# Filter stage: the other half's ten columns, dealt out in runs of lines instead of by rows

## The chip, the cores and the metric

The kernel runs on one core of a Trainium2 chip. The metric is the time of one execution on the device, in microseconds (us); several executions are timed and the median is given. Engines are named as in the profile: PE (TensorE), DVE (VectorE), ACT (ScalarE), POOL (GpSimd) and SP (SyncE, here the main issuer of DMAs). PEld is the loading of weights into TensorE.

## What is computed

The input is `x` of 16 samples, 32 channels and 64 x 64 pixels. Four residual layers follow each other, each on a group-normalised copy of `x`: an attention layer with 3x3 and 7x7 convolutions, a convolution quantised to 8 bits, a depthwise 3x3 convolution with kernels made from the pooled input, and an oriented filter. The change lies in the last one. Cut to that layer:

```python
center_k, surround_k = _make_kernels()      # 8 orientations each, 21 x 21 Gaussians, sigma 3.65 and 3.65/8; surround 3 times wider
tidx = jnp.arange(16) % 8                   # sample n has orientation n % 8
center_resp   = per_sample_conv(x, center_k[tidx])
surround_resp = per_sample_conv(x, surround_k[tidx])
return jnp.maximum(center_resp - lstd * surround_resp, 0.0)   # lstd: scaled local deviation of x
```

Every channel of a sample is convolved with the same 21x21 kernel, so a pixel needs the values up to ten rows and ten columns away.

## The kernel before, in words

**Layout.** Partitions hold 4 image rows modulo 4 (G) times 32 channels; the free dimension holds the 16 samples. The filter stage turns this around: for each sample the image is transposed into `xt[s]`, where the 128 partitions are 4 rows x 32 columns (one half of the width), and the free dimension holds half, high and low part (each value is two float16), 22 row blocks of 4 rows (16 real ones and 3 of padding on each side) and 32 channels. A filter is then a set of matmuls. The weights, 128 x 128, say how the pixels of one block of 4 rows x 32 columns enter the pixels of another, and one matmul applies them to up to 16 row blocks x 32 channels = 512 columns. Three matmuls (high x high, high x low, low x high) make one product of nearly float32 precision.

**Windows.** The weights come in ten windows for each kernel (centre and surround, `f`) and orientation `t`. Windows 0 to 4 are the own half, row blocks -2 to 2 (`rows_of`, L1747). Window 5 is the outer rows, from the tile `outer`. Windows 6 to 9 are the neighbour columns: of the other half, the ten columns next to the border reach over, with seven row blocks. These are 240 pairs of row and column for each half; they are gathered in the tile `edges[s]` as two parts of 120 partitions, near and far (windows 6 and 7 for half 0, 8 and 9 for half 1; `rest_of`, L1757). In the kernel before, the near part is row blocks 1 to 3 and the far part is 4, 5, half of 6 and half of 0, each with all ten columns, in every orientation. A window whose weights are all zero is skipped (`filled`, L1749 and L1760).

**How the edges come there.** The ten columns lie on other partitions, and each is needed shifted by several row blocks. So `store_edges` (L481) writes them with 8 DMAs of 10 partitions to the DRAM tensor `edge_columns`, as 40 lines (row of the block x column) per half, and `load_edges` (L496) or `load_right` (L1365) reads them back with 7 DMAs per half, of 40 or 20 lines, each line as two pieces of 1 KB. `copy_outer` (L490) fills `outer` with 2 DMAs.

**Order of the work.** Samples are taken in the order n = 2t + s: the two samples of orientation t, then the next orientation. Everything with index s has two buffers. TensorE's `filters(t, s)` (L1738) does the rows of both kernels and halves, waits for `outer`, the left and the right edges, and then does the rest. The last sample is split by halves. VectorE transposes (`turn_in`), makes the low part (`low`) and combines the results (`combine`); ScalarE makes the high part (`high`), normalises and takes roots. `high` for sample n waits until sample n - 2 is filtered.

**The DMA queues.** SP issues, in order: the table of orientation 0 and then, for sample 0, stores, outer copies and the loads of *both* halves (L536 to L539), the same for sample 1 (L542), and the table of orientation 1 (L543). Then a loop (L545) over orientations: for s = 0 and 1 `prefetch(t + 1, s)`, which loads only the left half, and `store_out(t, s)`; then `load_tables(t + 2)`. From orientation 1 on the right half is loaded by ScalarE's own DMA queue, in `load_right`, which stands between ScalarE's activations in its loop (L1397). A DMA issued there holds up the activations behind it. TensorE waits on counts of DMAs, 16 for each (L1773 to L1775).

Of the kernel before, what the change touches and what calls it, by code (L numbers as in the profile page):

```python
# [20 lines left out]
B, C, H, W = 16, 32, 64, 64  # L21
P = 128
G = 4
NY = H // G
# [15 lines left out]
KSZ, NT = 21, 8  # L40
NH = W // 2
YP, YN = 3, NY + 6
# [8 lines left out]
NREAL = 12 * NBW  # L51

KB, KQ, KV, KK = range(4)
NSIDE, NCENT = 256, 640


def host_constants():
# [15 lines left out]
    j, wi = p // NBW, p % NBW  # L73
    real = p < 12 * NBW
    rows_in, cols_in, used = [], [], []
    for d in range(-2, 3):
        rows_in.append(4 * d + r), cols_in.append(w), used.append(p >= 0)
    rows_in.append(np.where(r < 2, 12 + r, r - 12)), cols_in.append(w), used.append(p >= 0)
    neighbour_rows = np.array([[4 * a + q - 12 for a in (1, 2, 3) for q in range(4)],
                               [4 * a + q - 12 for a in (4, 5) for q in range(4)] + [12, 13, -10, -9]])  # L80
    for hf in range(2):
        for part in range(2):
            rows_in.append(neighbour_rows[part][np.minimum(j, 11)])
            cols_in.append(NH + wi if hf == 0 else wi - NBW)
            used.append(real)
    tab = np.zeros((NT, P, 2, NWIN, 2, P), np.float16)
    for t in range(NT):
        th = float(np.float32(t * np.pi / NT))
        xr = xx * np.cos(th) + yy * np.sin(th)
        yr = -xx * np.sin(th) + yy * np.cos(th)  # L90
        for cs, m in enumerate((1.0, 3.0)):
            k = np.exp(-0.5 * (xr * xr / (3.65 * m) ** 2 + yr * yr / (3.65 / 8 * m) ** 2))
            k = k / k.sum() * TS
            for v in range(NWIN):
                dh = rows_in[v][:, None] - r[None] + 10
                dw = cols_in[v][:, None] - w[None] + 10
                ok = (dh >= 0) & (dh < KSZ) & (dw >= 0) & (dw < KSZ) & used[v][:, None]
                m_ = np.where(ok, k[np.clip(dh, 0, 20), np.clip(dw, 0, 20)], 0.0)
                hi = m_.astype(np.float16)
                tab[t, :, cs, v, 0] = hi  # L100
                tab[t, :, cs, v, 1] = (m_ - hi.astype(np.float64)).astype(np.float16)
# [32 lines left out]
def program(nc, x, conv_w, pack, m1, mb1, dyn_w, cf, ch, tables, out):  # L134
# [3 lines left out]
    with ctx:  # L138
# [248 lines left out]

        @block.sync
        def _(sp):
# [91 lines left out]
            def store_edges(t, s):  # L481

                wait_alone(sp, g.xl, 2 * t + s + 1)
                for h, w0 in ((0, 0), (1, NH - NBW)):
                    for r in range(G):
                        sp.dma_start(edge_dram[s, h, NBW * r:NBW * r + NBW],
                                     xt[s][NH * r + w0:NH * r + w0 + NBW, 1 - h].rearrange("p l y c -> p l (y c)")
                                     ).then_inc(edge_out[s], 16)
# [7 lines left out]
            def load_edges(t, s, halves=(0,)):  # L496
                sp.wait_ge(edge_out[s], 128 * (t + 1))
                for h in halves:
                    for part, at_, r0, n, a in ((0, 0, 0, 4, 1), (0, 4, 0, 4, 2), (0, 8, 0, 4, 3),
                                                (1, 0, 0, 4, 4), (1, 4, 0, 4, 5), (1, 8, 0, 2, 6), (1, 10, 2, 2, 0)):  # L500
                        sp.dma_start(edges[s][NBW * at_:NBW * (at_ + n), part, h],
                                     edge_dram[s, h, NBW * r0:NBW * (r0 + n), :, C * a:C * (a + NY)]
                                     ).then_inc((edge_in if h == 0 else right_in)[s], 16)
# [41 lines left out]
            with sp.Fori(0, (NT - 2) // 2) as t2:  # L545
                for slot in range(2):
                    t = 2 * t2 + slot
                    for s in range(2):
                        prefetch(t + 1, s)
                        store_out(t, s)  # L550
                    load_tables(t + 2, slot)
# [602 lines left out]
        def _(a):  # L1154
# [210 lines left out]
            def load_right(t, s):  # L1365
                a.wait_ge([g.edge_out0, g.edge_out1][s], 128 * (t + 1))
                for part, at_, r0, n, y in ((0, 0, 0, 4, 1), (0, 4, 0, 4, 2), (0, 8, 0, 4, 3),
                                            (1, 0, 0, 4, 4), (1, 4, 0, 4, 5), (1, 8, 0, 2, 6), (1, 10, 2, 2, 0)):
                    a.dma_start(edges[s][NBW * at_:NBW * (at_ + n), part, 1],
                                edge_dram[s, 1, NBW * r0:NBW * (r0 + n), :, C * y:C * (y + NY)]  # L1370
                                ).then_inc([g.right_in0, g.right_in1][s], 16)
# [25 lines left out]
            with a.Fori(0, NT - 2) as t:  # L1397
# [85 lines left out]
        def _(pe):  # L1483
# [254 lines left out]
            def filters(t, s):  # L1738
# [18 lines left out]
                def rest_of(f, hf):  # L1757
                    for window, src in ((5, outer[s][:, hf]), (6 + 2 * hf, edges[s][0:NREAL, 0, hf]),
                                        (7 + 2 * hf, edges[s][0:NREAL, 1, hf])):
                        if not filled[t, f, window]:  # L1760
                            continue
                        for lt, lx in ((0, 0), (0, 1), (1, 0)):
                            rows = src.shape[0]
                            last = mm(bank[4 * s + 2 * f + hf], tb[0:rows, f, window, lt], src[:, lx],  # L1764
                                      start=False, stop=(window == 7 + 2 * hf and lt == 1), skip_group_check=True)
# [8 lines left out]
                pe.wait_ge([g.edge_in0, g.edge_in1][s], 16 * 7 * (t + 1))  # L1774
                pe.wait_ge([g.right_in0, g.right_in1][s], 16 * 7 * (t + 1))  # L1775
# [77 lines left out]
```

## Time and profile before

| | |
|---|---|
| median of 3 runs | 1197.33 us (1196.41 to 1201.05) |
| the profiled execution's own time | 1200.27 us |
| its span, first to last instruction | 1197.3 us |
| mean granted TensorE clock | 0.961 of full speed |
| TensorE matmul busy | 90% of the span |
| VectorE, ScalarE, GpSimd busy | 68%, 45%, 27% |
| filter stage on the chain of waits | from 887.6 us to the end |

Busy shares are averages over five stages with different limits; for one stage the chain of waits and the stretches are to be read. Times in the trace count from the first instruction. A DMA's row on a queue (SPq, ACTq) is the time for which the issuing queue was taken up, not the transfer.

### The profile page before, as it was taken

To read this page: it belongs to the slowest core of one execution; us is meant where nothing else is said; L and a number is where in the kernel's file an instruction comes from. 1 tells how busy PE (TensorE), PEld (TensorE's weight loads), DVE (VectorE), ACT (ScalarE), POOL (GpSimd) and SP (SyncE) were. 2 spreads that over 40 slices of the span, in tenths; PEclk is the share of its full clock that TensorE was granted. 3 is DMA by queue.
4 is the path that set the end of the run, shared out by engine and by line. 5 is a ranking of instruction groups with operands and counts; after the bars stand their busy time and mean duration, and the time that the engine had idled before them with its cause. 6 is when DMAs were issued, how large, how long until landed. Compare 5 with 4: busy or idle time off the path is not lost.

```text
span 1197.3 us, 38501 instructions
## 1 busy us (share of the span) xinstructions
PE 1076.6 (90%) x17036; PEld 790.9 (66%) x17036; DVE 808.9 (68%) x1001; ACT 537.1 (45%) x747; POOL 321.8 (27%) x364
## 2 busy tenths in 40 slices
PE   2999999999999999999923589978989999999997
PEld 2999989999899999999821245433334444444443
DVE  6456585684857848477296978689989645466444
ACT  3524635546364563625334967677941212121110
POOL 1374545535464363545410000022300000000000
PEclk9999999999999999999956988989989999999999
DMA  6020020200202000010001444322354654566551
GB/s 210 7 77 3 3 76 3 76 3 3 76 3 76 3 18 27 3 42 3 3 1 37 105 104 112 91 59 71 93 140 124 190 171 117 171 178 187 152 139 43
DMA packets 52115, 89.77 MB, mean 75 GB/s; under 512 B 8795, under 2 KB 36699, under 8 KB 50940
## 3 DMA queue, kind: packets, MB, share of 16 engines
q1 hardware_dynamic: 44264, 80.56, 24.3%
q10 hardware_dynamic: 7700, 6.89, 2.0%
q8 instruction: 133, 2.18, 0.7%
q14 instruction: 18, 0.15, 0.0%
HBM read 36.89 MB, written 11.99 MB: 41 GB/s over the span
## 4 chain that ended last, share of the span: by engine, by line
PE 74%; DVE 17%; ACT 3%; issue 3%; DMA 2%; SPq 1%; DVEq 0%; ACTq 0%
PE psum L1519 38%; PE psum L1753 16%; PE psum L1764 10%; PE psum L1653 5%; DVE small L711 2%; PE psum L1555 2%; DMA arena<-arena 2%; DVE arena L1008 1%; DVE small L586 1%; DVE X L904 1%; PE psum L1568 1%; DVE arena L1027 1%; DVE arena L1015 1%; PE psum L1541 1%; DVE arena L1021 1%
## 5 line engine op out<-in xcount | busy, mean ns | idle before, releaser
L1519 PE MATMUL psum<-arena 128*128 128x64 f16 (+2 forms) x11904 | 514.9, 207 | 22.3 <-DMA arena<-arena 12.6
L1519 PEld LDWEIGHTS psum<-arena 128*128 128x128 f16 x11904 | 497.8, 99 | 38.2 <-issue 12.7
L625 DVE TENSOR_TENSOR arena<-psum,arena 128x512 f32<-128x512 f32 x128 | 87.9, 691 | 170.0 <-PE psum L1519 142.4
L1753 PE MATMUL psum<-arena 128*128 128x512 f16 (+2 forms) x936 | 192.4, 366 | 0.0
L1753 PEld LDWEIGHTS psum<-arena 128*128 128x128 f16 x936 | 92.2, 99 | 98.7 <-issue 3.3
L1431 POOL TENSOR_SCALAR arena<-arena,constants_f 128x256 f16<-128x256 f16 x126 | 138.6, 1128 | 0.0
L1427 POOL TENSOR_TENSOR arena<-arena 128x256 f16<-128x256 f32 x63 | 51.7, 820 | 309.5 <-ACT arena L1189 309.5
L1184 ACT ACTIVATE arena<-arena 128x256 f16<-128x256 f32 x63 | 26.5, 420 | 208.4 <-issue 105.5
L1764 PE MATMUL psum<-arena 120*128 120x512 f16 (+1 forms) x528 | 116.9, 379 | 0.0
L1764 PEld LDWEIGHTS psum<-arena 120*128 120x128 f16 (+1 forms) x528 | 51.4, 97 | 61.8
L1475 POOL TENSOR_TENSOR arena<-arena 128x1024 f32<-128x1024 f32 x16 | 30.4, 1899 | 206.8 <-ACT arena L1331 153.9
L1653 PE MATMUL psum<-arena 128*32 128x512 f16 x1152 | 69.6, 404 | 6.3 <-DMA arena<-arena 6.3
L1188 ACT ACTIVATE arena<-arena,small,constants_f 128x256 f16<-128x256 f32 x126 | 74.9, 663 | 0.0
L1043 DVE TENSOR_TENSOR arena<-arena 128x1024 f16<-128x1024 f32 x16 | 19.6, 1223 | 74.9 <-ACT arena L1359 74.6
L1363 ACT ACTIVATE arena<-arena 128x1024 f32<-128x1024 f32 x16 | 16.9, 1057 | 109.3 <-DVE arena L1051 109.3
L1359 ACT ACTIVATE arena<-arena 128x1024 f16<-128x1024 f32 x16 | 16.9, 1055 | 108.3 <-PE psum L1764 97.3
L1653 PEld LDWEIGHTS psum<-arena 128*32 128x32 f16 x1152 | 32.4, 101 | 42.0 <-DMA arena<-arena 7.7
L1432 POOL TENSOR_TENSOR arena<-arena 128x256 f32 (+1 forms) x63 | 55.7, 884 | 0.0
L1210 ACT ACTIVATE arena<-arena,small,constants_f 128x2048 f16<-128x2048 f32 x14 | 37.7, 2757 | 37.7 <-DVE arena L683 37.7
L688 DVE SCALAR_TENSOR_TENSOR arena<-arena,constants_f 128x2048 f16<-128x2048 f32 x14 | 38.2, 2730 | 15.7 <-ACT arena L1210 15.7
L1702 PE MATMUL psum<-arena,constants_f 128*128 128x512 f16 x192 | 47.0, 397 | 0.6 <-DVE arena L1008 0.4
L1555 PE MATMUL psum<-arena 128*128 128x64 f16 x768 | 25.8, 198 | 21.5 <-DVE arena L666 21.5
(209 smaller groups left out, 1413.3 us busy)
## 6 DMA issues: line engine op xcount, KB each, us to landing
arena<-in_filter_tables SPq DMA_DIRECT2D x8, 1280.0 KB, 8.6
arena<-arena SPq DMA_DIRECT2D x32, 264.0 KB, 3.9
X<-in_x SPq DMA_DIRECT2D x16, 512.0 KB, 4.7
arena<-arena SPq DMA_DIRECT2D x32, 256.0 KB, 4.0
out<-X SPq DMA_DIRECT2D x16, 512.0 KB, 4.0
arena<-edge_columns SPq DMA_DIRECT2D x90, 80.0 KB
arena<-edge_columns ACTq DMA_DIRECT2D x70, 80.0 KB
arena<-arena SPq DMA_DIRECT2D x32, 140.0 KB, 2.5
```

The costliest lines, as they stand in the source:

```text
L625: v.tensor_tensor(out_, bank_rows(k), biasrow, ALU.add).then_inc([g.staged0, g.staged1][k], 1)
L688: v.scalar_tensor_tensor(PX[1][:, :, :, s], p_ch, smask[s], PX[0][:, :, :, s], ALU.mult, ALU.subtract).then_inc(g.pl_ready, 1)
L1188: a.activation(k_rows(0, y2, s), chunk(y2, KK), ACT.Identity, scale=smask[s], bias=zero1)
L1427: gp.tensor_tensor(khl[:, y2 % 2, 1], chunk(y2, KK), khl[:, y2 % 2, 0], ALU.subtract).then_inc(g.klow, 1)
L1431: gp.tensor_scalar(k_rows(1, y2, s), khl[:, y2 % 2, 1], smask[s], None, ALU.mult)
L1432: gp.tensor_tensor(v_rows(1, i, y2), chunk(y2, KV), v_rows(0, i, y2), ALU.subtract).then_inc(g.lo_ready, 1)
L1519: last = mm(conv[k][:, c0:c1], win[:, kk, lx, y + e, dx:dx + W, :].rearrange("p w s -> p (w s)"), wt[:, lw, d, w0:w1], start=(n == 0), sto ...
L1555: last = mm(att[:, H * c:H * c + H], PX[lp][:, c].rearrange("p h s -> p (h s)"), VV[lv][:, kk * C + c], start=(c % 8 == 0 and n == 0), sto ...
L1653: last = mm(slot_banks(B + n)[hf][C * row:C * row + C, :], kw[:, lw, row, dx], src[:, k, lx, 8 * hf + e:8 * hf + e + 8, dx:dx + W], start= ...
L1702: mm(bank[4 * k + hf], near, wx3[k][:, l, 8 * hf:8 * hf + 8, dx:dx + W], start=(dx + l == 0), stop=False, skip_group_check=True)
L1753: mm(bank[4 * s + 2 * f + hf][:, C * lo:C * hi], tb[:, f, d + 2, lt], xt[s][:, hf, lx, YP + d + lo:YP + d + hi].rearrange("p y c -> p (y c)"),
L1764: last = mm(bank[4 * s + 2 * f + hf], tb[0:rows, f, window, lt], src[:, lx], start=False, stop=(window == 7 + 2 * hf and lt == 1), skip_gr ...
```

## The change

The 40 lines of a half are put into `edge_columns` by column first in orientations 0, 1 and 7 (`BY_COLUMN`), by row otherwise, and in orientations 5 to 7 with the rows mirrored. For each orientation a table (`EDGE_NEAR`, `EDGE_FAR`; orientations 5 to 7 use those of 3 to 1, mirrored) says which runs of lines of which row block belong to the near part and which to the far part. A part has 112 to 128 rows instead of 120. In orientations 2 and 6 the division stays as before. The loads follow the tables, one DMA for each entry; an entry with five numbers gathers several short runs in one DMA with a source of four levels. TensorE's waits count the loads so far. Since the number of loads differs from one orientation to the next, the loops over orientations on SP and ScalarE are written out.

```diff
+BY_COLUMN = (0, 1, 7)
+EDGE_NEAR = {
+    0: ((1, 0, 20), (2, 0, 20), (3, 0, 20), (4, 0, 20), (5, 0, 20), (0, 2, 2, 0, 5), (6, 0, 2, 0, 5)),
+    1: ((1, 0, 8), (2, 0, 12), (3, 0, 20), (4, 0, 28), (5, 0, 30), (6, 0, 2, 0, 7)),
+    2: ((1, 0, 40), (2, 0, 40), (3, 0, 40)),
+    3: ((2, 20, 15), (3, 0, 40), (4, 0, 40), (5, 0, 30)),
+    4: ((2, 10, 30), (3, 0, 40), (4, 0, 40), (5, 0, 10)),
+}
+EDGE_FAR = {
+    0: ((1, 20, 20), (2, 20, 20), (3, 20, 20), (4, 20, 20), (5, 20, 20), (0, 2, 2, 5, 5), (6, 0, 2, 5, 5)),
+    1: ((0, 2, 2, 0, 10), (1, 8, 32), (2, 12, 28), (3, 20, 20), (4, 28, 12), (5, 30, 10), (6, 0, 2, 7, 3)),
+    2: ((4, 0, 40), (5, 0, 40), (6, 0, 20), (0, 20, 20)),
+    3: ((0, 20, 20), (1, 0, 40), (2, 0, 20), (2, 35, 5), (5, 30, 10), (6, 0, 20)),
+    4: ((0, 20, 20), (1, 0, 40), (2, 0, 10), (5, 10, 30), (6, 0, 20)),
+}
+
+def edge_line(t, row, column):
+    row = G - 1 - row if t > NT // 2 else row
+    return G * column + row if t in BY_COLUMN else NBW * row + column
...
+        def edge_pieces(t, s, h):
+            line = 2 * YN * C
+            for k, part in enumerate(edge_parts(t, h)):
+                at_ = 0
+                for a, lines in part:
+                    n = sum(len(run) for run in lines)
+                    src = edge_dram[s, h, lines[0][0]:lines[0][-1] + 1, :, C * a:C * (a + NY)]
+                    if len(lines) > 1:
+                        src = bass.AP(edge_dram.tensor, src.offset,
+                                      [[G * line, len(lines)], [line, len(lines[0])], [YN * C, 2], [1, C * NY]])
+                    yield edges[s][at_:at_ + n, k, h], src
+                    at_ += n
+
+        def edge_loads(t, h):
+            return 16 * sum(len(part) for turn in range(t + 1) for part in edge_parts(turn, h))
...
-                        sp.dma_start(edge_dram[s, h, NBW * r:NBW * r + NBW],
+                        first, last = edge_line(t, r, 0), edge_line(t, r, NBW - 1)
+                        sp.dma_start(edge_dram[s, h, first:last + 1:(last - first) // (NBW - 1)],
...
-                    for part, at_, r0, n, a in ((0, 0, 0, 4, 1), (0, 4, 0, 4, 2), (0, 8, 0, 4, 3),
-                                                (1, 0, 0, 4, 4), (1, 4, 0, 4, 5), (1, 8, 0, 2, 6), (1, 10, 2, 2, 0)):
-                        sp.dma_start(edges[s][NBW * at_:NBW * (at_ + n), part, h],
-                                     edge_dram[s, h, NBW * r0:NBW * (r0 + n), :, C * a:C * (a + NY)]
-                                     ).then_inc((edge_in if h == 0 else right_in)[s], 16)
+                    for dst, src in edge_pieces(t, s, h):
+                        sp.dma_start(dst, src).then_inc((edge_in if h == 0 else right_in)[s], 16)
...
-            with sp.Fori(0, (NT - 2) // 2) as t2:
-                for slot in range(2):
-                    t = 2 * t2 + slot
-                    for s in range(2):
-                        prefetch(t + 1, s)
-                        store_out(t, s)
-                    load_tables(t + 2, slot)
+            for t in range(NT - 2):
+                for s in range(2):
+                    prefetch(t + 1, s)
+                    store_out(t, s)
+                load_tables(t + 2, t % 2)
...
+                for dst, src in edge_pieces(t, s, 1):
+                    a.dma_start(dst, src).then_inc([g.right_in0, g.right_in1][s], 16)
...
-            with a.Fori(0, NT - 2) as t:
+            for t in range(NT - 2):
...
-                    for window, src in ((5, outer[s][:, hf]), (6 + 2 * hf, edges[s][0:NREAL, 0, hf]),
-                                        (7 + 2 * hf, edges[s][0:NREAL, 1, hf])):
-                        if not filled[t, f, window]:
-                            continue
+                    near, far = (edge_count(part) for part in edge_parts(t, hf))
+                    used = [v for v in (5, 6 + 2 * hf, 7 + 2 * hf) if filled[t, f, v]]
+                    for window in used:
+                        rows = {5: P, 6 + 2 * hf: near, 7 + 2 * hf: far}[window]
+                        src = outer[s][:, hf] if window == 5 else edges[s][0:rows, (window - 6) % 2, hf]
...
-                pe.wait_ge([g.edge_in0, g.edge_in1][s], 16 * 7 * (t + 1))
-                pe.wait_ge([g.right_in0, g.right_in1][s], 16 * 7 * (t + 1))
+                pe.wait_ge([g.edge_in0, g.edge_in1][s], edge_loads(t, 0))
+                pe.wait_ge([g.right_in0, g.right_in1][s], edge_loads(t, 1))
```

An entry of three numbers is (row block, first line, lines); one of five is (row block, first row, rows, first column, columns). The weights in the tables of constants are arranged to match.

## Rows read from the trace of the kernel before

**Rows 1.** The page, part 1: busy time, share of the span, instructions of each engine.

```profile
PE 1076.6 (90%) x17036; PEld 790.9 (66%) x17036; DVE 808.9 (68%) x1001; ACT 537.1 (45%) x747; POOL 321.8 (27%) x364
```

**Rows 2.** The chain that ended last, in time order: start us, us, what.

```profile
887.61 14.24 PE psum L1753 x60
901.85 7.79 PE psum L1764 x36
...
929.41 11.99 PE psum L1753 x60
941.40 7.78 PE psum L1764 x36
...
1020.50 6.48 PE psum L1764 x30
...
1038.98 6.49 PE psum L1764 x30
...
1187.44 3.90 PE psum L1764 x18
```

**Rows 3.** Stretches of the filter stage: first and last of five of 50 us.

```profile
core 0: us, PE busy (x) PEld busy (x) DVE busy (x) ACT busy (x) POOL busy (x), PEclk, DMA share, GB/s
900.00:950.00 50.00, 50.00 (x243) 23.57 (x242) 39.36 (x54) 7.64 (x8) 0.00 (x0) 1.00 0.52 140
...
1100.00:1150.00 50.00, 50.00 (x244) 23.72 (x243) 25.32 (x23) 7.54 (x7) 0.00 (x0) 1.00 0.55 158
```

**Rows 4.** Timeline of SP's queue, samples 0 and 1: start us, us, what.

```profile
888.09 11.70 SPq L501 DMA_DIRECT2D arena<-edge_columns  x14
899.99 2.92 SPq L486 DMA_DIRECT2D edge_columns<-arena  x8
902.96 1.43 SPq L492 DMA_DIRECT2D arena<-arena  x2
```

**Rows 5.** Groups by line and shape, from 860 us: count | busy us, mean ns.

```profile
L1764 PE MATMUL psum<-arena 120*128 120x512 f16 x384 | 91.8, 379 | 0.0
...
L1764 PE MATMUL psum<-arena 128*128 128x512 f16 x144 | 39.0, 379 | 0.0
```

**Rows 6.** L501: all durations, then its fifth to eighth issue alone.

```profile
L501 SPq DMA_DIRECT2D arena<-edge_columns x126: 769/781/1076, 888.1 to 1164.0; - x126
...
891.60 0.77 SPq L501 DMA_DIRECT2D arena<-edge_columns  x1
...
892.42 0.78 SPq L501 DMA_DIRECT2D arena<-edge_columns  x1
...
893.24 0.77 SPq L501 DMA_DIRECT2D arena<-edge_columns  x1
...
894.06 0.78 SPq L501 DMA_DIRECT2D arena<-edge_columns  x1
```

**Rows 7.** Other lines of SP's queue: ns min/median/max; under L520, L478 their landing.

```profile
L486 SPq DMA_DIRECT2D edge_columns<-arena x128: 281/329/1682, 882.6 to 1156.9; - x128
...
L520 SPq DMA_DIRECT2D arena<-arena x128: 548/591/1309, 780.8 to 881.9; - x128
...
DMA to landing us min/median/max: 1.9/2.0/5.8
...
L478 SPq FUSED_REGOPS  x6: 43/43/43, 949.4 to 1126.0; - x6
...
DMA to landing us min/median/max: 5.5/8.6/9.7
```

**Rows 8.** Stretches around the first filter matmul; columns as in rows 3.

```profile
882.00:886.50 4.50, 0.23 (x2) 0.00 (x0) 0.63 (x1) 1.26 (x2) 0.00 (x0) 0.86 0.90 303
886.50:891.80 5.30, 5.23 (x13) 1.94 (x14) 4.01 (x4) 0.00 (x0) 0.00 (x0) 0.50 0.60 140
```

**Rows 9.** Timeline of one sample's round on ScalarE: start us, us, what.

```profile
1008.61 1.06 ACT L1359 ACTIVATE arena<-arena 128x1024 f16<-128x1024 f32 x1 [10.31 <-PE psum L1764]
...
1017.03 1.06 ACT L1363 ACTIVATE arena<-arena 128x1024 f32<-128x1024 f32 x1 [6.23 <-DVE arena L1051]
...
1017.03 5.62 ACTq L1369 DMA_DIRECT2D arena<-edge_columns  x7
```

More of the change, by code:

```diff
@@ L50, with edge_parts, edge_count, edge_rows @@
 NPS = 3
-NREAL = 12 * NBW
 KB, KQ, KV, KK = range(4)
 NSIDE, NCENT = 256, 640
+BY_COLUMN = (0, 1, 7)
+EDGE_NEAR = {
[5 rows of a table added]
+}
+EDGE_FAR = {
[5 rows of a table added]
+}
+def edge_line(t, row, column):
+    row = G - 1 - row if t > NT // 2 else row
+    return G * column + row if t in BY_COLUMN else NBW * row + column
+def edge_parts(t, hf):
+    parts = []
+    for part in (EDGE_NEAR[min(t, NT - t)], EDGE_FAR[min(t, NT - t)]):
+        pieces = []
+        for a, *of in part:
+            if len(of) == 2:
+                lines = [range(of[0], of[0] + of[1])]
+                if hf:
+                    lines = [range(40 - of[0] - of[1], 40 - of[0])]
+            else:
+                r0, c0 = of[0], of[2]
+                if hf:
+                    r0, c0 = G - of[0] - of[1], NBW - of[2] - of[3]
+                lines = [range(G * c + r0, G * c + r0 + of[1]) for c in range(c0, c0 + of[3])]
+            pieces.append((6 - a if (t > NT // 2) != (hf == 1) else a, lines))
+        parts.append(pieces)
+    return parts
+def edge_count(part):
+    return sum(len(run) for a, lines in part for run in lines)
+def edge_rows(t, part):
+    place = {edge_line(t, q, c): (q, c) for q in range(G) for c in range(NBW)}
+    at = [(4 * (a - 3) + place[n][0], place[n][1]) for a, lines in part for run in lines for n in run]
+    return np.array(at).T
 def host_constants():
@@ L72, in host_constants @@
     r, w = p // NH, p % NH
-    j, wi = p // NBW, p % NBW
-    real = p < 12 * NBW
     rows_in, cols_in, used = [], [], []
@@ L78, in host_constants @@
     rows_in.append(np.where(r < 2, 12 + r, r - 12)), cols_in.append(w), used.append(p >= 0)
[L79 to L85, printed above, removed]
     tab = np.zeros((NT, P, 2, NWIN, 2, P), np.float16)
@@ L90, in host_constants @@
         yr = -xx * np.sin(th) + yy * np.cos(th)
+        del rows_in[6:], cols_in[6:], used[6:]
+        for hf in range(2):
+            for part in edge_parts(t, hf):
+                rows, cols = edge_rows(t, part)
+                unused = np.zeros(P - len(rows), int)
+                rows_in.append(np.concatenate([rows, unused]))
+                cols_in.append(np.concatenate([cols, unused]) + (NH if hf == 0 else -NBW))
+                used.append(p < len(rows))
         for cs, m in enumerate((1.0, 3.0)):
@@ L1366, in load_right @@
                 a.wait_ge([g.edge_out0, g.edge_out1][s], 128 * (t + 1))
[L1367 to L1371, printed above, removed]
+                for dst, src in edge_pieces(t, s, 1):
+                    a.dma_start(dst, src).then_inc([g.right_in0, g.right_in1][s], 16)
             a.wait_ge(g.zero3, 1)
@@ L1757, in rest_of @@
                 def rest_of(f, hf):
-                    for window, src in ((5, outer[s][:, hf]), (6 + 2 * hf, edges[s][0:NREAL, 0, hf]),
-                                        (7 + 2 * hf, edges[s][0:NREAL, 1, hf])):
-                        if not filled[t, f, window]:
-                            continue
+                    near, far = (edge_count(part) for part in edge_parts(t, hf))
[3 more added lines that the diff above has]
+                        src = outer[s][:, hf] if window == 5 else edges[s][0:rows, (window - 6) % 2, hf]
                         for lt, lx in ((0, 0), (0, 1), (1, 0)):
-                            rows = src.shape[0]
                             last = mm(bank[4 * s + 2 * f + hf], tb[0:rows, f, window, lt], src[:, lx],
-                                      start=False, stop=(window == 7 + 2 * hf and lt == 1), skip_group_check=True)
+                                      start=False, stop=(window == used[-1] and lt == 1), skip_group_check=True)
                     return last
```

## The prediction

> **What bounds the kernel now.** I read the page first. TensorE is busy 90% of the span [rows 1], so the question is what it does in the stage that the change touches, and whether it ever waits there. The chain of waits in order of time answers both: from 887.61 to 1191.34 us it holds nothing but filter matmuls, L1753 and L1764 by turns, one pair for each of fifteen samples and two for the last, which is split by halves [rows 2]. Between 900 and 1150 us every 50 us stretch has 50.00 us of TensorE, at a granted clock of 1.00 (2.4 GHz), while VectorE has 25 to 39 us, ScalarE under 8 and the DMA engines a share of about 0.5 (first and last of the five stretches [rows 3]). So a matmul less is time less, for as long as everything that feeds the matmuls stays early. The feeders were read next, in the timeline of SP's queue, since it is SP that brings the neighbour columns. At the start of the stage SP has no slack at all: it issues sample 0's fourteen edge loads from 888.09 for 11.70 us, to 899.79, and TensorE wants them at 901.85 [rows 2, 4].
>
> **What goes.** With the columns dealt out in runs, the centre kernel of six orientations (0, 1, 3, 4, 5, 7) has no weight in the far window. I counted this from the formula of the kernels: before, all four edge windows of both kernels held weights in all eight orientations. A window costs three matmuls, there are two halves, so a sample of these orientations loses 6, twelve samples lose 72. The chain gives 36 matmuls of L1764 in 7.78 us and 30 in 6.48 [rows 2]: 0.216 us each, 1.30 per sample, **15.6 us** in all, and all of it on the path. The rows of a matmul change from 120 to between 112 and 128; with 120 and with 128 one reads 379 ns [rows 5], so this costs nothing.
>
> **What comes: loads.** The bytes are the same (240 rows of two 1 KB pieces per half). The number of loads is not: counted from the tables, a half takes 14, 13, 7, 10, 9, 10, 7, 13 loads in orientations 0 to 7, where each took 7. What does an issue cost? L501 has 126, with 769/781 ns at least and in the median [rows 6]. The decisive reading is that this doesn't follow the size: of SP's first seven, the fifth moves 40 rows and takes 0.77 us, the sixth and the seventh move 20 rows and take 0.78 and 0.77, the eighth has 40 again and 0.78; from start to start it is 0.82 [rows 6]. In orientation 0, 10 of the 14 loads of a half are exactly this 20-row form. The other four gather 10 rows in five runs, a four-level source that no row shows. From below it is bounded by a store of 10 rows, 329 ns, from above by the dearest L501, 1076 ns [rows 6, 7]; I take 0.83 us from start to start as for the others, being the nearest in direction and shape.
>
> **What comes: the stores.** Still 8 per sample, 10 rows each, but in orientations 0, 1 and 7 the DRAM side is strided. Now 329 ns (2.92 us for 8). A gain is excluded, for the rows and bytes are the same. From above, a 32-row copy strided on both sides takes 591 ns [rows 7], which is 0.26 more each. I take 0, as the nearest row is the store itself, and keep up to 2.1 us per sample for the range.
>
> **The loops that go.** SP's and ScalarE's loops over orientations become straight code. A register instruction between the issues takes 43 ns [rows 7]; I cost it at nothing. What hides it is the slack of both queues in the steady stage, reckoned below.
>
> **On the path: the start of the stage.** Both halves of samples 0 and 1 are loaded by SP alone, so SP issues 28 loads where it issued 14, twice. By the trace's own clock:
> - Sample 0: 28 loads from 888.09 end near 911.4; the last starts at 910.5 and lands 2.0 us later (the median of the nearest copies, L520 [rows 7]), at 912.5. TensorE, ready at 901.85, waits about 10.7 us.
> - The clock then falls. After the idle stretch from 882 to 886.5 us, the granted clock was 0.50 (1.2 GHz) for 886.5 to 891.8 [rows 8], and the first 60 filter matmuls took 14.24 us where later ones take 11.99 [rows 2]: 2.3 us lost. I take 2.3 for each stall, and 0 to 3 for the range. Sample 0 ends at 912.5 + 6.5 + 2.3 = 921.3, and sample 1's own rows are done at 933.3.
> - SP goes on only now: 8 stores and 2 copies of sample 1 (2.92 + 1.43 us [rows 4]) from 911.5, the wait for their landing (0.4), and 28 loads from 916.3 to 939.5, landed at 940.7. TensorE waits 7.4 us. The loss of the first stall is inside this one: the path is SP's.
> - Sample 1 ends at 940.7 + 6.5 + 2.3 = 949.5. Before, sample 2 began at 929.41 [rows 2]. **Behind by 20.1 us**, the two samples' own saving counted already.
>
> **Behind it.** Table 1 is issued at 939.8 and takes 8.6 us (9.7 at most [rows 7]): 948.4, just ahead of 949.5. Sample 2's 13 loads per half come from both queues in parallel: SP 940.2 + 2.9 + 1.4 + 0.5 + 13 x 0.87 = 956.3, landed 957.6, wanted at 949.5 + 12.0 = 961.5. ScalarE's `high` for sample 3 stands behind its own 13 issues and comes at 955.8, not 949.5; VectorE's low half, the combination of sample 1, the clamp and the root follow, as now in 8.4 us from 1008.61 to 1017.03 [rows 9], then 13 issues of 0.80, landed near 977, wanted at 980. Table 2 would be there at 983.7, wanted at 986.5. Three covers of 3 to 4 us each; none gives way by these numbers.
>
> In steady state ScalarE's round, `high` to the last load, is 14.0 us with 7 issues (1008.61 to 1022.65 [rows 9]) and 14.0 + 0.80 x 3 or 6 with 10 or 13, so 16.4 and 18.8. Samples last 17.2 to 19.8 us, but only 13.6 in orientation 4. There ScalarE falls behind by some 2 to 6 us; the loads it issues until 1022.65 land some 2 us later and are wanted at 1038.98 [rows 2, 9], 14 us later still, so TensorE doesn't see it. SP's round is 4.4 + 0.9 + 13 x 0.87 + 0.8 = 17.4 us at most, below ScalarE's.
>
> **Sum.** +20.1 from samples 0 and 1, -13.0 from the other ten samples: **+7.1 us**. The sum is made against the profiled execution, whose span is 1197.3 and whose time is 1200.27 us, 2.9 above the median of the three runs, 1197.33. I add the difference to the median: 1204.4.
>
> **A rule against the reading.** A 20-row load holds its queue for 0.78 us [rows 6]. The Trainium skill, "DMA: Bandwidth & Descriptors", section "Issuing engines are not separate DMA queues", says that the time on the sequencer to start a DMA is usually small relative to the DMA itself, and its section "Anatomy of one DMA" puts the dispatch at about 50 ns within a fixed cost that is mostly completion. By it twice as many loads would cost nothing, and the time would be 1181.7. This trace speaks against that for this form of load.
>
> **Rivals.**
> 1. *Issue time follows the size, so nothing is late.* Half-size loads at half the time keep SP's 11.7 us per sample; the whole 15.6 us is gained: 1197.3 - 15.6 = **1181.7**. For it: stores of 10 rows take 329 ns. Against: 20 and 40 rows alike. This is the rival of the other side; it decides when a 20-row load costs under some 0.45 us. 0.12. The skill's rule above gives the same end.
> 2. *The unseen four-level loads are cheap.* At 0.37 us from start to start, 8 in each set of 28 save 3.7 us, 7.4 over the two sets: 1197.0, **no change**. For it the stores' 10 rows, against it that rows haven't mattered so far. 0.14.
> 3. *The start is dearer and drags a second thing along.* Strided stores at 0.59 (+4.2 us) and four-level loads at 1.08 (+0.25 x 16 = +4) put SP 8 us later, table 1 with it: **1212**; and the covers of 3 us at samples 3 and 4 go. 0.14.
> 4. *That the change doesn't do what it says* (the far window still filled) is excluded by the count.
>
> **Chances.** Forecast 0.60, the rivals 0.12, 0.14, 0.14. A measurement here tells 0.5%, 6 us: faster is below 1191.3, slower above 1203.3. The forecast has a width of about 3 us around 1204.4, so 0.18 of its 0.60 counts as no change; of rival 2's 0.14, 0.12 does. Faster 0.12; same 0.18 + 0.12 = 0.30; slower 0.42 + 0.02 + 0.14 = 0.58. The range leaves out rival 1 and reaches from rival 2 to rival 3 with its own spread: 1196 to 1214.
>
> **What would show it.** In the profile after: L1764's successor with 1392 - 936 = 456 matmuls; TensorE waiting on a DMA of the edge tiles twice, by 11 and 7 us, ahead of samples 0 and 1, with the clock at half after each; SP's load line with 56 issues before table 1, over 23 us per set; no wait of TensorE from sample 2 on. Wrong it is if SP's loads in that place are clearly under 0.77 us, or if a third wait stands among the samples.

## The result, and the profile after

The changed kernel takes 1210.53 us in the median (1207.9 to 1216.49, 7 runs), beside 1196.41 for the kernel before (1191.15 to 1201.05, 7 runs): a ratio of 1.0134, 95% interval 1.0098 to 1.0169, so 12 to 20 us slower. (The ratio is that of the compared sets of runs; the quotient of the two medians is 1.0118. The same holds for the experiments below, each of which was compared with runs of the kernel before taken beside it.) The forecast was 1204.4, 7.1 us more than before, in a range of 1196 to 1214. The sign is as forecast, and so is the mechanism at the start of the stage; the loss is about twice what was summed, because further waits came behind the start.

Where one execution is compared with another I use the filter stage alone, from the start of its first matmul to the start of its last: 887.4 to 1190.9 before, 880.0 to 1202.3 after, **303.5 and 322.3 us**. The code ahead of it is the same in both, and yet the profiled executions of all the kernels here reach it between 880.0 and 887.4 us; that scatter of 7 us is in the spans, but not in the stage. Each kernel was profiled once, so how much the stage itself varies from one execution to the next was not measured.

The page, part 1, of the changed kernel (as rows 1):

```profile
PE 1057.1 (87%) x16964; PEld 777.3 (64%) x16964; DVE 809.0 (67%) x1001; ACT 537.1 (44%) x747; POOL 322.8 (27%) x364
```

72 matmuls fewer, as counted (17036 - 16964), but TensorE's share fell from 90% to 87%. The stretches of its filter stage (columns as in rows 3) say where it now stands still:

```profile
core 0: us, PE busy (x) PEld busy (x) DVE busy (x) ACT busy (x) POOL busy (x), PEclk, DMA share, GB/s
900.00:950.00 50.00, 37.09 (x155) 16.29 (x156) 21.88 (x38) 4.51 (x5) 0.00 (x0) 0.82 0.36 97
950.00:1000.00 50.00, 45.44 (x211) 20.97 (x210) 28.62 (x26) 9.74 (x9) 0.00 (x0) 0.93 0.55 153
1000.00:1050.00 50.00, 50.00 (x244) 23.63 (x243) 26.30 (x24) 8.67 (x8) 0.00 (x0) 1.00 0.56 167
...
1100.00:1150.00 50.00, 48.00 (x234) 22.62 (x233) 29.92 (x27) 9.74 (x9) 0.00 (x0) 1.00 0.60 168
```

The timeline of SP's queue, ScalarE's queue (ACTq) and TensorE at the start of the stage; the bracket is TensorE's idle time and what ended it (as rows 4; L1814 is `rows_of`, L1825 `rest_of`, L569 and L1432 are the loads, L555 the stores, L561 the outer copies, L546 the tables):

```profile
880.42 23.50 SPq L569 DMA_DIRECT2D arena<-edge_columns  x28
904.45 3.10 SPq L555 DMA_DIRECT2D edge_columns<-arena  x8
905.62 9.49 PE L1825 MATMUL psum<-arena 128*128 128x512 f16 x30 [11.45 <-DMA arena<-edge_columns]
...
909.07 23.67 SPq L569 DMA_DIRECT2D arena<-edge_columns  x28
914.94 12.15 PE L1814 MATMUL psum<-arena 128*128 128x512 f16 x60
...
932.79 0.43 SPq L546 DMA_DIRECT2D arena<-in_filter_tables  x1
933.36 3.42 SPq L555 DMA_DIRECT2D edge_columns<-arena  x8
934.39 8.76 PE L1825 MATMUL psum<-arena 128*128 128x512 f16 x30 [7.29 <-DMA arena<-edge_columns]
936.83 1.43 SPq L561 DMA_DIRECT2D arena<-arena  x2
940.59 11.03 SPq L569 DMA_DIRECT2D arena<-edge_columns  x13
940.60 11.53 ACTq L1432 DMA_DIRECT2D arena<-edge_columns  x13
...
954.98 6.65 PE L1825 MATMUL psum<-arena 128*128 128x512 f16 x30
...
960.65 11.05 ACTq L1432 DMA_DIRECT2D arena<-edge_columns  x13
...
970.99 0.71 SPq L546 DMA_DIRECT2D arena<-in_filter_tables  x1
...
978.18 9.05 PE L1825 MATMUL psum<-arena 128*128 128x512 f16 x30 [4.56 <-DMA arena<-edge_columns]
```

28 loads take 23.50 and 23.67 us of SP where 14 took 11.70. TensorE waits 11.45 us in sample 0, 7.29 in sample 1, and again, unforeseen, 4.56 in sample 3. The 30 matmuls behind each of these waits take 9.49, 8.76 and 9.05 us; undisturbed, in sample 2, they take 6.65. That is the clock: in the changed kernel's stretches around the first wait (PEclk is the granted clock),

```profile
900.00:905.50 5.50, 0.00 (x0) 0.00 (x0) 5.50 (x6) 0.00 (x0) 0.00 (x0) 0.50 0.17 43
905.60:911.00 5.40, 5.38 (x13) 1.89 (x14) 4.17 (x22) 0.73 (x2) 0.00 (x0) 0.50 0.53 115
911.00:915.00 4.00, 4.00 (x19) 1.76 (x18) 2.06 (x2) 0.53 (x1) 0.00 (x0) 0.95 0.32 81
```

TensorE is idle in the first, runs at 0.50 (1.2 GHz) in the second, 13 matmuls in 5.4 us, and is nearly back at full speed in the third (0.95). Two later waits complete the list, in the timeline of TensorE: at sample 12, for its table, and at the last sample.

```profile
1124.74 12.15 PE L1814 MATMUL psum<-arena 128*128 128x512 f16 x60 [2.00 <-issue]
...
1190.08 3.40 PE L1825 MATMUL psum<-arena 128*128 128x512 f16 x15 [1.15 <-DMA arena<-edge_columns]
```

The first of these two has no releaser in the trace. That it is the table is worked out: SP issues the table of orientation 6 at 1113.97, the longest time from issue to landing of any table here is 10.7 us, and TensorE goes on at 1124.74.

The account: 303.5 - 15.6 (matmuls) + 26.5 (11.45 + 7.29 + 4.56 + 2.00 + 1.15, waits) + 7.4 (2.84 + 2.11 + 2.40, clock) = 321.8, against 322.3 measured.

### The profile page after: what moved, and what is told of

Same layout as the page of the kernel before. It is cut to its first block, busy times and chain, and to the rows that moved or that the text cites. A ratio compares the mean times of both kernels' runs of the same rounds, so it can differ in the third digit from the quotient of the medians.

```text
span 1208.7 us, 38329 instructions
## 1 busy us (share of the span) xinstructions
PE 1057.1 (87%) x16964; PEld 777.3 (64%) x16964; DVE 809.0 (67%) x1001; ACT 537.1 (44%) x747; POOL 322.8 (27%) x364
## 4 chain that ended last, share of the span: by engine, by line
PE 52%; DVE 22%; ACTq 7%; SPq 7%; issue 5%; DMA 4%; ACT 4%; DVEq 0%
PE psum L1580 36%; ACTq L1432 7%; PE psum L1714 5%; SPq L569 4%; PE psum L1814 3%; PE psum L1825 3%; DVE small L775 2%; DMA edge_columns<-arena 2%; PE psum L1616 2%; SPq L555 2%; DVE arena L1072 1%; DVE small L650 1%; DVE arena L1079 1%; PE psum L1629 1%; DVE arena L1091 1%
## 5 line engine op out<-in xcount | busy, mean ns | idle before, releaser
L1814 PE MATMUL psum<-arena 128*128 128x512 f16 (+2 forms) x936 | 192.1, 366 | 2.0 <-issue 2.0
L1814 PEld LDWEIGHTS psum<-arena 128*128 128x128 f16 x936 | 92.1, 98 | 100.7 <-issue 5.6
L1825 PE MATMUL psum<-arena 128*128 128x512 f16 (+4 forms) x456 | 108.7, 398 | 24.4 <-DMA arena<-edge_columns 24.4
L1248 ACT ACTIVATE arena<-arena 128x256 f16<-128x256 f32 x63 | 26.5, 420 | 204.8 <-issue 105.5
L1825 PEld LDWEIGHTS psum<-arena 128*128 128x128 f16 (+4 forms) x456 | 45.8, 101 | 84.3 <-issue 36.0
L1714 PE MATMUL psum<-arena 128*32 128x512 f16 x1152 | 66.3, 391 | 6.1 <-DMA arena<-arena 6.1
L1763 PE MATMUL psum<-arena,constants_f 128*128 128x512 f16 x192 | 44.5, 382 | 0.8 <-DVE arena L1072 0.7
```

The costliest lines, as they stand in the source:

```text
L1714: last = mm(slot_banks(B + n)[hf][C * row:C * row + C, :], kw[:, lw, row, dx], src[:, k, lx, 8 * hf + e:8 * hf + e + 8, dx:dx + W], start= ...
L1814: mm(bank[4 * s + 2 * f + hf][:, C * lo:C * hi], tb[:, f, d + 2, lt], xt[s][:, hf, lx, YP + d + lo:YP + d + hi].rearrange("p y c -> p (y c)"),
```

## The experiments

The theory after the result: (A) at the start, the number of loads issued by the one queue costs; (B) the third wait is something else, made by orientation 1's 13 loads and by the tables that SP issues next to the stores and the last loads. Rivals: issue time follows the size; the number or the traffic of the transfers costs, wherever they are issued; the written-out loops cost. In all of them "stage" is the stretch defined above.

**1. The kernel before with the first loads cut in two.** Orientation 0 only; no matmul goes.

```diff
+                    if cut:      # cut = len(halves) == 2: samples 0 and 1
+                        whole = [(part, at_ + k * n // 2, r0 + k * n // 2, n // 2, a)
+                                 for part, at_, r0, n, a in whole for k in range(2)]
```

> The kernel before; only each edge load that SP issues for samples 0 and 1 is cut in two (20 + 20 and 10 + 10 lines), so 28 loads of the same bytes for a sample, no matmul less. If the count of issues costs the time: SP's 28 loads take about 23.4 us instead of 11.7, TensorE waits about 11 us in sample 0 and 7 us in sample 1, the clock loses 2.3 to 2.8 us after each; some 22 us slower, ratio to before 1.018 (1.015 to 1.021). If issue time follows the size of a load: 28 loads take about 12 us, no wait, ratio 1.000.

Measured: 1215.62 us, ratio 1.0208 (1.0166 to 1.0250), stage 325.7 us, 22.2 more than before. Its timeline (L506 the loads, L1769 `rest_of`):

```profile
881.26 23.42 SPq L506 DMA_DIRECT2D arena<-edge_columns  x28
...
906.28 10.40 PE L1769 MATMUL psum<-arena 128*128 128x512 f16 x36 [12.19 <-DMA arena<-edge_columns]
...
934.23 10.09 PE L1769 MATMUL psum<-arena 128*128 128x512 f16 x36 [5.56 <-DMA arena<-edge_columns]
```

The same bytes in twice the loads hold SP for 23.42 us, and the two waits appear in a kernel that has nothing else of the change. (A) is shown, and that the size of a load sets its issue time is refuted for loads of 10 to 40 lines.

**2. Orientation 0 by rows.** In the changed kernel the tables of orientation 0 are those of orientation 2.

```diff
-BY_COLUMN = (0, 1, 7)
+BY_COLUMN = (1, 7)
-    0: ((1, 0, 20), (2, 0, 20), (3, 0, 20), (4, 0, 20), (5, 0, 20), (0, 2, 2, 0, 5), (6, 0, 2, 0, 5)),
+    0: ((1, 0, 40), (2, 0, 40), (3, 0, 40)),
...
+    0: ((4, 0, 40), (5, 0, 40), (6, 0, 20), (0, 20, 20)),
```

> The changed kernel, but orientation 0 keeps the division by rows: 14 loads for each of samples 0 and 1, and their 12 matmuls come back (+2.6 us). If the start is what costs: the two waits of 11.4 and 7.3 us and both clock losses go, and as SP and ScalarE aren't late at sample 3, most of its wait of 4.6 too; 10 samples save 13.0 us, so ratio to before 0.989 to 0.992. If the other orientations' 9 to 13 loads, the strided stores or the written-out loops cost as much: ratio 1.00 or above.

Measured: 1188.76 us, ratio 0.9957 (0.9934 to 0.9979), stage 299.8. Half a miss, the ratio lies above the 0.989 to 0.992 expected: the first two waits are gone (0.66 us is left), but not the third:

```profile
939.61 6.65 PE L1825 MATMUL psum<-arena 128*128 128x512 f16 x30 [0.38 <-DMA arena<-edge_columns]
...
956.63 0.64 SPq L546 DMA_DIRECT2D arena<-in_filter_tables  x1
959.67 3.37 SPq L555 DMA_DIRECT2D edge_columns<-arena  x8
...
963.50 8.54 PE L1825 MATMUL psum<-arena 128*128 128x512 f16 x30 [5.25 <-DMA arena<-edge_columns]
```

So the wait in sample 3 doesn't come from the late start. It belongs to orientation 1 and to what stands next to its last loads. The chain of waits has this for the last of the 13 loads on ScalarE's queue, from its start to the landing:

```profile
956.37 6.99 DMA arena<-edge_columns
```

SP issues the output store at 956.20 and the table at 956.63. With the 2.39 us that such a load takes in the next experiment, where no table is near, it would have been there at 958.8, and TensorE, ready at 958.25, would have waited some 0.5 us instead of 5.25 (an estimate from these rows).

**3. The right halves of samples 0 and 1 on ScalarE's queue.** All 28 loads stay.

```diff
-            load_edges(0, 0, (0, 1))
+            load_edges(0, 0)
...
             normalise(1, 0)
+            a.wait_ge(g.s3x, B)
+            load_right(0, 0)
+            a.wait_ge(g.s3q, B)
+            load_right(0, 1)
```

> The changed kernel, but the right halves of samples 0 and 1 are loaded from ScalarE's queue, which has nothing to do there; the number of loads stays. If it is the one queue's issue time: SP's 14 loads take 11.7 us, the waits of 11.4 and 7.3 us fall to under 1 us each, both clock losses go, about 23 us back: ratio to before 0.990 to 0.998, the lower end if sample 3's wait goes too. If it is the number of transfers itself (landing, traffic), wherever they are issued: waits stay within 2 us of the changed kernel's, ratio 1.013.

Measured: 1192.13 us, ratio 0.9992 (0.9961 to 1.0024), stage 297.0. The stage gives back 25.3 us, where about 23 were expected; the ratio is just above the expected 0.990 to 0.998. The profiled execution is the shortest of the ten (1185.95; they go up to 1199.02), and the 13 us between them are more than the 7 us of scatter ahead of the stage, so the stage of this one may be shorter than is usual for this kernel. The same number of transfers from two queues leaves 1.21 us of the first wait and nothing of the second. So it is the one issuing queue that is the limit, not the traffic. In place of the wait in sample 3 stands one in sample 2, as its timeline shows (L1829 `rest_of`):

```profile
895.83 6.65 PE L1829 MATMUL psum<-arena 128*128 128x512 f16 x30 [1.21 <-DMA arena<-edge_columns]
...
923.95 11.05 SPq L569 DMA_DIRECT2D arena<-edge_columns  x13
924.84 10.68 ACTq L1432 DMA_DIRECT2D arena<-edge_columns  x13
...
937.26 9.17 PE L1829 MATMUL psum<-arena 128*128 128x512 f16 x30 [3.86 <-DMA arena<-edge_columns]
```

and its chain of waits has for the last of these loads on ScalarE's queue:

```profile
934.74 2.39 DMA arena<-edge_columns
```

**4. The tables right after the second sample's stores.**

```diff
                 for s in range(2):
-                    prefetch(t + 1, s)
+                    store_edges(t + 1, s)
+                    copy_outer(t + 1, s)
+                    if s:
+                        load_tables(t + 2, t % 2)
+                    load_edges(t + 1, s)
                     store_out(t, s)
-                load_tables(t + 2, t % 2)
```

The table of orientation 1 is moved in the same way.

> The changed kernel, but SP issues the tables of orientations 1 to 7 right after the stores and outer copies of the second sample instead of after its loads and the output store. If the table in flight is what held up the stores' landing (4 to 6 us) and the last load's landing (7.1 us): the stores land in about 2.5 us in all samples but those whose copies it follows, the wait of 4.6 us in sample 3 with its clock loss of 2.5 goes, and the wait of 2.0 us at sample 12 for its table; the first two waits stay at 11.4 and 7.3; 7 to 9 us back, ratio to before 1.006. If only the number of issues counts: nothing changes, 1.013.

Measured: 1205.99 us, ratio 1.0115 (1.0067 to 1.0163), stage 312.6, which is 9.7 less than the changed kernel's. The ratio doesn't bear the expectation out: its interval leaves out the 1.006 expected, holds the 1.013 of the other case and overlaps the changed kernel's. What speaks for (B) is the trace of one execution. Of its waits only the first two are left, 11.49 and 8.82 us; those in samples 3, 12 and 15 are gone. The second has grown by 1.5, since the loads now stand behind a table. So the order of the tables makes the wait in sample 3; in whole runs the gain is too small to be told from noise. How near a table has to be isn't settled: in experiment 3 the table stands 0.45 us behind the last load of sample 3 (953.94), and TensorE, ready at 958.26, didn't wait, so that load landed within 4.3 us.

**5. Both together.** Edits 3 and 4.

> Both earlier edits together: right halves of samples 0 and 1 on ScalarE's queue, and the tables issued right after the second sample's stores. If the two causes are what is left (SP's issue time at the start; tables ahead of stores and last loads): only waits of under 1.5 us remain, filter stage from its first to its last matmul 288 to 291 us (303.5 in the kernel before, 322.3 in the changed one), ratio to before 0.987 to 0.991. If ScalarE's round of 13 loads holds TensorE up by itself in orientation 1 or 7: a wait of 3 us or more stays there, stage 293 us or more, ratio 0.993 or more.

Measured: 1186.05 us, ratio 0.9927 (0.9906 to 0.9949), stage 296.0. The second case: one wait of 3.87 us stays in sample 2, with its clock loss (1.00 and 0.68 us elsewhere). So something holds orientation 1 up that neither edit touches.

**6. Merged loads.** Loads of equal runs from neighbouring row blocks become one DMA with a source of four levels.

```diff
+                    elif blocks > 1:
+                        src = bass.AP(edge_dram.tensor, src.offset,
+                                      [[C, blocks], [line, len(lines[0])], [YN * C, 2], [1, C * NY]])
```

> The changed kernel with the loads of equal runs from neighbouring row blocks made one DMA with a four-level source (same rows and bytes, rows of a part in another order): 6, 13, 4, 9, 8, 9, 4, 13 loads for a half in orientations 0 to 7. SP issues 12 loads for each of samples 0 and 1. If an issue costs 0.8 us whatever its size: SP's 12 loads take about 10 us, the waits of 11.4 and 7.3 us go; orientation 1's wait of 4 to 5 us with its clock loss stays, since its 13 loads and the tables stay where they were; stage about 295 to 297 us, ratio to before 0.993 to 0.997. If a merged load costs by its rows (100 for 20): its issue takes 4 us, SP's start isn't shorter, stage about 320 us, ratio 1.013.

Measured: 1228.41 us, ratio 1.0280 (1.0244 to 1.0316), stage 338.4. At the start it did what (A) says: in orientation 0, where five blocks of 20 lines are merged, 12 loads took 9.75 us, and TensorE had no wait in samples 0 and 1. But orientations 2 to 6, where neighbouring blocks are merged too, two or three of them, became much dearer: TensorE waits 5.30 us in sample 4, 4.27 in sample 8, 2.81 in sample 10 and 7.51 in sample 12, where the changed kernel has only the 2.00 for a table. Smaller waits stand between, and 5.96 in the last sample. The chain of waits of this kernel, for the four loads of a sample of orientation 2, and SP's own waits in the stage:

```profile
984.88 0.81 SPq L587
...
985.74 1.07 SPq L587
...
986.86 0.69 SPq L587
...
987.60 7.22 SPq L587
```

```profile
SPq L587 <- DMA edge_columns<-arena: 55.5, 11, 10.1
```

The fourth load has 20 lines, and it is the one that is held for 7.22 us, behind the two merged ones (120 and 80 lines). That the queue was full is my reading; the trace doesn't show it. And SP waited 55.5 us in all for its stores to land (17.9 in the changed kernel). The Trainium skill, "DMA: Bandwidth & Descriptors", section "Why a DMA increments its semaphore by 16 and not by 1", says that a transfer is spread over the largest number of engines up to 16 that divides the slowest dimension of both sides. By that rule, as an estimate, the merges of three, two and five blocks would use 3, 2 and 5 engines, and a 40-line load 10. The times don't contradict it (the 80 lines merged from two blocks are dearer than the 100 lines merged from five, so size alone isn't the cause), but no run here shows the number of engines itself, and none varied it alone. That it is the cause isn't shown.

**7. Merged loads with edits 3 and 4.**

> All three edits together. If the causes are known: no wait of over 1 us in the filter stage, stage 288 to 290 us against 303.5 before, the whole of the 15.6 us gained, ratio to before 0.986 to 0.990. If something else in the changed kernel costs (rows of 112 to 128, strided stores, straight-line code): stage above 292 us.

Measured: 1217.19 us, ratio 1.0184 (1.0154 to 1.0213), stage 325.4. A miss: waits of 3.30, 6.75, 4.52 and 5.92 us in samples 2, 4, 9 and 12, and up to 2.01 elsewhere, all on the edges. The one in sample 2 is that of experiment 5, since orientation 1 has nothing to merge; the other three are in orientations with merged loads, as in experiment 6.

**8. The kernel before with its loops written out.** `for t in range(NT - 2)` in place of the two loops, nothing else.

> The kernel before with SP's and ScalarE's loops over orientations written out, nothing else. By the theory that only issues and tables count: stage 303.5 us within 0.5, ratio 1.000 within the interval. If fetching straight-line code holds up the queues: waits appear, stage over 305 us.

Measured: 1198.09 us, ratio 1.0001 (0.9976 to 1.0025), stage 303.5, the same as before to the tenth. Straight-line code costs nothing here.

**9 to 11. Merging in orientation 0 alone.** The first with orientation 1 by rows and the tables moved, the second without the edit to orientation 1, the third without the moved tables.

```diff
-            if of_part and len(lines) == 1 and of_part[-1][2] == lines and of_part[-1][0] + of_part[-1][1] == a:
+            if t == 0 and of_part and len(lines) == 1 and of_part[-1][2] == lines and of_part[-1][0] + of_part[-1][1] == a:
...
+def table_of(t):
+    return 2 if t == 1 else min(t, NT - t)
```

> The changed kernel with three edits: only orientation 0's five loads of equal runs merged into one (6 loads a half), orientation 1 by rows (7 loads, its 12 matmuls back, 2.6 us), tables right after the second sample's stores. By the theory that an issue costs 0.8 us and that merged loads are cheap where they use 5 engines and dear where they use 2 or 3: no wait over 1 us, stage 290.5 to 292 us (303.5 before, 13.0 saved), ratio to before 0.989 to 0.992. If merging costs in orientation 0 too, or moving the tables costs elsewhere: a wait of 2 us or more, stage over 293.5 us.

> As the one before, but orientation 1 keeps its 13 loads in runs. Its first sample's loads can't start before ScalarE and VectorE, busy until about 918 us, have made that sample; theory: 13 issues then end 5 us later than 7, which leaves a wait of 3 to 4 us and a clock loss of 2.5 us in sample 2, stage 293.5 to 295 us, ratio 0.992 to 0.996. If that wait came from traffic of the start's many loads or of the table: it is gone here, stage 288 to 289 us, ratio 0.986 to 0.989.

> The first of these three with the tables where they were. Theory: with 7 loads in orientations 1 and 2 the queues aren't late, and a table issued after the output store no longer collides with stores or last loads in samples 2 to 5; stage within 1.5 us of the first one's, at most a wait of 1 to 2 us at sample 12 for its table and 1 us at sample 15. If tables ahead of stores cost by themselves: waits of over 3 us among samples 2 to 5.

| edits | median, us | ratio (95%) | stage, us | waits over 0.5 us |
|---|---|---|---|---|
| merged 0, rows 1, tables | 1184.14 | 0.9915 (0.9895 to 0.9936) | 290.4 | none |
| merged 0, tables | 1187.78 | 0.9949 (0.9930 to 0.9968) | 294.0 | 3.76 in sample 2, 0.51 in sample 3 |
| merged 0, rows 1 | 1181.58 | 0.9912 (0.9892 to 0.9932) | 292.3 | 0.80 in sample 2, 0.92 in the last |

The first two came out as expected to 0.1 us, and the third lies 1.9 us above the first, 0.4 beyond the 1.5 expected. Orientation 1's price is the difference of the first two: its 13 loads cost 3.6 us of stage more than the 12 matmuls (2.6 us) that they save. Why neither queue edit helps it is in the timeline of the second, where SP has nothing to do when sample 2's stores come at last:

```profile
916.97 1.04 ACT L1446 ACTIVATE arena<-arena 128x1024 f16<-128x1024 f32 x1
...
919.44 1.23 DVE L1130 TENSOR_TENSOR arena<-arena 128x1024 f16<-128x1024 f32 x1 [0.24 <-DVE arena L1141]
...
920.77 2.95 SPq L573 DMA_DIRECT2D edge_columns<-arena  x8
...
925.23 11.10 SPq L587 DMA_DIRECT2D arena<-edge_columns  x13
...
940.47 8.33 PE L1848 MATMUL psum<-arena 128*128 128x512 f16 x30 [3.76 <-DMA arena<-edge_columns]
```

Sample 2's `high` (L1446) is made at 916.97, when VectorE is through with the extremes of the local variance and ScalarE with the root behind them. From there the chain is stores, 13 loads on each queue (SP until 936.33, ScalarE until 938.28) and their landing, after which TensorE goes on at 940.47, while its own rows are done at 936.7. ScalarE begins 1.6 us after SP (926.85 beside 925.23), because its loads stand behind a root (L1450, 926.84) that waits for VectorE; the loads ahead of that root, or more of them on SP, might take part of the 3.76 us away. No run tried it. With 7 loads, in the first of the three, the queues are through at 932.0 and 933.6, and TensorE waits 0.21 us.

The third shows that a table issued after the output store does little harm by itself (1.9 us of stage, none in the ratio). The large waits beside a table, 4.56 and 5.25 us, were in kernels with 13 loads in orientation 1, where little time is left behind the last load.

## Why the prediction was right in kind and low in size

| term of the sum | forecast, us | measured, us |
|---|---|---|
| 72 matmuls | -15.6 | 72 fewer |
| 28 loads of SP, twice | 23.3 and 23.2 | 23.50 and 23.67 |
| wait in sample 0, clock | 10.7 + 2.3 | 11.45 + 2.84 |
| wait in sample 1, clock | 7.4 + 2.3 | 7.29 + 2.11 |
| sample 2 begins later by | 20.1 | 21.2 |
| sample 3 | 0 | 4.56 + 2.40 |
| table, sample 12 | 0 | 2.00 |
| last sample | 0 | 1.15 |

**What bounds the kernel, the matmuls and the start** were right. The reading that carried the forecast, that 20 lines and 40 lines hold the queue for the same 0.78 us [rows 6], was put to the test by itself in the first experiment and held. The four-level loads that no row had shown cost 0.76 to 0.81 us, as assumed (the sixth and seventh issue of the changed kernel, in SP's timeline):

```profile
884.77 0.81 SPq L569 DMA_DIRECT2D arena<-edge_columns  x1
...
885.62 0.76 SPq L569 DMA_DIRECT2D arena<-edge_columns  x1
```

The strided stores cost next to nothing: eight of them took 3.10 us in sample 1, where it had been 2.92 [rows 4]. Rival 1 (issue time by size) is refuted for these loads by the first experiment, and with it the time of 1181.7 us. The Trainium skill, "DMA: Bandwidth & Descriptors", section "Issuing engines are not separate DMA queues", calls the time to initiate a DMA usually small relative to the DMA itself; here 14 more issues on one queue cost 11.7 us. The section "Anatomy of one DMA", which the prediction sets beside it, is about DMAs issued from GpSimd, and these came from SP, so its 50 ns was no measure for them. Rival 2 (cheap four-level loads) is refuted by the two rows above. The loops were rightly costed at nothing (experiment 8).

**The step that failed** is "Three covers of 3 to 4 us each; none gives way by these numbers". A third wait among the samples was the prediction's own sign of being wrong, and it came. The cover at sample 3 was reckoned with edges landed near 977, wanted at 980. Put on the same clock (7.4 us are added, since the changed kernel's stage begins at 880.0 instead of 887.4), they landed at 985.5, wanted at 981.0. Three terms of it were too small, and the chain of waits of the changed kernel has the two large ones:

```profile
936.42 4.16 DMA edge_columns<-arena
...
970.92 7.13 DMA arena<-edge_columns
```

Sample 2's stores took 4.16 us to land, 2.3 us beyond the end of the outer copies at 938.26; I had allowed 0.5. The last load of sample 3, on ScalarE's queue, took 7.13 us from its start to landing where I took 2.0 from rows 7, a row of other copies on a quiet queue. ScalarE's 13 issues took 11.53 in sample 2, not 10.4. Together 8 us, against a cover of 3. The landing is the term that decides: with 2.4 us, as in experiment 3, that load would have been there at 973.3 on the changed kernel's clock, and TensorE was ready at 973.62 (an estimate). In both places SP issues a table of 1280 KB next to it, 0.57 us ahead of the stores (932.79) on the same queue, and 0.07 us behind the start of that load (970.99) on the other queue; with the tables elsewhere the wait is gone (experiment 4). The trace of before could have told it: there too a table was issued 3 us ahead of sample 4's stores,

```profile
949.58 0.38 SPq L478 DMA_DIRECT2D arena<-in_filter_tables  x1
...
956.23 1.43 SPq L492 DMA_DIRECT2D arena<-arena  x2
...
961.27 5.87 SPq L501 DMA_DIRECT2D arena<-edge_columns  x7
```

and the loads began 3.6 us after the copies' end at 957.66. In sample 10, behind the table issued at 1059.84, it was 2.4 us; in the other samples from 2 on it is 0.04 to 0.23. I had summed the issue times of the queues, not what was in flight. Table 6's late landing (2.00 us, sample 12) is a like omission: "There ScalarE falls behind by some 2 to 6 us" followed the edges and forgot the table, which stands behind the late output store. In the last sample the last load (1186.71) took 3.23 us to land instead of 2.0, which is about its wait of 1.15.

**Rival 3** named the right place, "the start is dearer and drags a second thing along", and its 1212 is near the result, but its cause was wrong: neither the stores' stride nor the four-level loads were dearer. The range's upper end, 1214, came from this rival, so that 1210.53 lies inside it is in part luck: the 18.8 us by which the stage grew, added to the 1197.33 from which the forecast starts, give 1216.1. That the late start drags sample 3 along is not so either: with an early start the wait there is as long (5.25 us, experiment 2).

## What to carry to other kernels

Where DMAs are small, cost them by their number per issuing queue, and do that first for the prologue, where one queue does what two do later and nothing has been fetched ahead; here the matmuls saved there were worth less (2.6 us for orientation 0) than the issues that saved them. A cover of a few us isn't safe if it was reckoned from landing times on a quiet queue: look for the large transfer that stands next to it. Apply a saving where there is slack for its price: with orientation 0's loads merged and orientation 1 left by rows the same idea gives 0.9912 (0.9892 to 0.9932) instead of 1.0134.

## What the runs showed of the hardware that wasn't expected

A merged load isn't cheap because it is one issue: with an outer dimension of 5 (100 lines) twelve loads went through SP in 9.75 us, while with outer dimensions of 3 and 2 (120 and 80 lines) the next issue on the queue was held for 7.22 us and SP waited up to 10.1 us for its stores to land. And the queue time of a load hardly depends on its size: 0.78 us in the median before with 20 and 40 lines [rows 6], 0.81 in the changed kernel with 5 to 40, 0.64 at least, whether its source has three levels or four; a store of 10 lines takes 0.33 us in the median and a whole table of 1280 KB mostly 0.38 to 0.88 (1.77 at most). What sets these levels stays open; no run varied it.
